# Slot attention in a decoder megakernel: the within-pair copies reordered, work moved between GpSimd and VectorE, and the lists of four engines rewritten

## The chip, the cores and the metric

The program runs on one core of one Trainium2 chip. The metric is the device time of one execution in microseconds, the median of three executions, and lower is better. A core has a matrix engine (TensorE, PE in the profile, with its weight loads as PEld), a vector engine (VectorE, DVE), an activation engine (ScalarE, ACT), a general engine (GpSimd, POOL), and SyncE (SP), whose queue issues the transfers from memory. Every engine has its own list of instructions, runs it in order, and waits for the others through semaphores. PSUM is the memory into which TensorE writes, here eight banks of 512 columns.

## What is computed

The program is two decoder layers; the change touches only the slot attention of the first. Cut to what matters:

```python
def step(carry, xs):                      # gsa2_scan, over t
    Sk, Sv = carry
    q_t, k_t, v_t, w_t, g_t, b_t = xs
    gt = jnp.exp(g_t)
    bw = b_t[:, :, None] * w_t
    Sk = Sk * gt[:, :, None, :] + k_t[..., :, None] * bw[:, :, None, :]
    Sv = Sv * gt[..., None] + bw[..., None] * v_t[:, :, None, :]
    s = jnp.einsum('bhd,bhdm->bhm', q_t, Sk) * SCALE
    a = jax.nn.softmax(s, axis=-1)
    o_t = jnp.einsum('bhm,bhmd->bhd', a, Sv)
...
q = short_conv(h @ Wq, cq)                # likewise k, v, w: 4 taps over t, then SiLU
g = jax.nn.log_sigmoid(h @ Wf1 @ Wf2)
w = l2norm(rs(w, M))
o = gsa2_scan(q, k, v, w, g, beta)
o = o * norm_w * jax.nn.sigmoid(gate)     # after a root-mean-square norm; then @ Wo
...
x = x + _L0_attn_ref(_layernorm(x, axis=-1), ...)
```

There are 64 sequences of 64 steps, 16 heads, and 128 channels and 128 slots per head.

## The kernel before, in words

The function `gsa` (from L754) holds the slot attention and takes the first 3600 us or so of the span. It goes through 16 heads with four **pairs** of token groups each, so 64 pairs. A pair has two halves, a and b, of 512 columns (eight sequences). The scan over 64 steps isn't run step by step. It is split by levels b = 1, 2, 4, 8, 16, 32: at level b the second run of b steps in each block of 2b is coupled to the first, so every level has its packed operands (P from the slot weights, G from the gates' decays), a product and a matmul. This happens twice in each half:

- **scores** (slots before the softmax): TensorE multiplies LT with AM at a level, VectorE multiplies the result in PSUM with G into TMP ("level product"), and a sum adds TMP to QK[0:512]. At levels 1, 2, 4 and 8 GpSimd does the sum (L1836, L1840, L1846, L1855 for b), at 16 and 32 VectorE (L1443, L1448). Then come transpose, maximum (L1457), its negative (nmx, L1459), Exp on ScalarE (L1715), and a custom instruction on VectorE (L1471).
- **kept attention** (after the softmax): a product AA times G gives AM at each level (VectorE L1479 to L1482 and L1487 for levels 1, 2, 8, 4, 16; GpSimd L1868 for level 32), TensorE multiplies it, and a predicated copy (L1486 to L1512 for b, L1353 to L1377 for a) puts the second runs of the result from PSUM under a mask into QK[512:1024]. Then TensorE reads the values (L1045 for a), ScalarE squares them, VectorE applies the gate (L1396), and the head's output is added to X (L1427, four instructions).

`packs`, `lefts` and `rights` are the access patterns of a level: 256 elements in the order (block, half, run of b). `rights` on QK or AA goes b elements in one region of 256, jumps to the other region, and so on; at b = 1 it jumps at every element. Besides, VectorE does the short convolutions (three instructions of 1008, 992 and 976 elements into CWV, L1399, L1405, L1415, and for CQK of 504, 496 and 488), and in-place products on GWV that prolong decays (`late`, `early`, for instance L1451 at level 2, L1433 at level 1). ScalarE starts each convolution from PSUM (L1661 for CWV), applies SiLU (L1653, L1654 into GWVa, that read CWV), packs P and G, and applies sigmoids, for which it changes its table of functions six times a pair.

The order is written out by hand. Every engine has a function `pair(h, gp, ...)` in which the statements of three pairs are interleaved: `within` (pair n, new projections), `before` (pair n-1: convolutions, gates) and `earlier` (pair n-2: scores and kept attention). The half's stages follow each other in a ring, half a pair apart. The first head and the last two pairs are unrolled; heads 1 to 15 are a loop `Fori`. SyncE loads a head's weights when the last reader of the old ones is through: WA (the four projections, 512 KB) after the last projection, WCV (taps), WFG (gates) and WO (output), each into its only buffer. The last reader of the old WA on TensorE is L1132, the first of the new one L1150. PSUM banks 0 to 3 serve half a, 4 to 7 half b.

## Time and profile before

| | |
|---|---|
| median of 3 executions | 5720.01 us (5716.29 to 5721.54) |
| the profiled execution | 5672.51 us, its span 5670.7 us |
| busy in the span: PE, DVE, ACT, POOL | 5100.0, 4610.0, 3778.8, 2229.3 us |
| granted TensorE clock | 0.97 of 2.4 GHz over the span, 0.99 from 300 to 3300 us |
| slot attention | about 80 to 3640 us of the span |

The page puts busy time beside the span for each engine; an instruction is named by its line, engine and operation, and by the tiles that it writes and reads. The profiled execution is 0.8% under the median; durations of single instructions come from it.

### The profile page before, as it was taken

The page shows a single profiled execution, that of the slowest core. Times are in us where ns is not written, and L with a number is a line of the kernel's source. Part 1 is how long each engine was busy: PE and PEld are TensorE (multiplying, and loading weights), DVE is VectorE, ACT ScalarE, POOL GpSimd, SP SyncE. Part 2 cuts the span into 40 slices and gives each one's busy share as a digit, 9 for nine tenths or more (in the row PEclk, how much of TensorE's full clock was granted, in tenths as well). Part 3 has the DMA queues.
Part 4 walks back from the last instruction along what each step waited for, and adds up shares of the span by engine and source line. Part 5 has one row for each costly group of instructions (what it writes and reads, how often), then busy time and mean ns, then how long its engine had stood idle before and what let it go on. Part 6 is the DMA issues. An engine that isn't in the chain of part 4 may idle for free. (4 is left out here: it accounts for less than half of the span.)

```text
span 5670.7 us, 113906 instructions
## 1 busy us (share of the span) xinstructions
PE 5100.0 (90%) x38178; PEld 3710.4 (65%) x38178; DVE 4610.0 (81%) x10272; ACT 3778.8 (67%) x9646; POOL 2229.3 (39%) x2774
## 2 busy tenths in 40 slices
PE   7898888988888988988988988787999999989999
PEld 4666666666666666666666666686865667768766
DVE  4999999999999999999999999687972238878623
ACT  4887787877887887877877878464861434446423
POOL 1454444554444544444544545243113320001252
PEclk9999999999999999999999999898999999999999
DMA  6300000000000000000000000001001238001134
GB/s 188 121 3 7 5 3 6 2 7 6 2 7 6 2 7 6 2 7 6 2 7 5 3 7 1 30 18 32 2 39 52 91 118 269 2 23 28 61 104 159
DMA packets 164355, 205.29 MB, mean 36 GB/s; under 512 B 22907, under 2 KB 149756, under 8 KB 163072
## 3 DMA queue, kind: packets, MB, share of 16 engines
q1 hardware_dynamic: 148016, 159.46, 9.1%
q0 software_dynamic: 12960, 34.63, 1.7%
q8 instruction: 347, 5.69, 0.4%
q10 hardware_dynamic: 2736, 3.09, 0.2%
q14 instruction: 296, 2.42, 0.1%
HBM read 158.33 MB, written 114.16 MB: 48 GB/s over the span
## 5 line engine op out<-in xcount | busy, mean ns | idle before, releaser
L1871 POOL TENSOR_TENSOR gsa_qka<-gsa_qka,gsa_tmpa 128x256 f32<-128x256 f32 x64 | 47.5, 742 | 444.5 <-DVE gsa_tmpa L1518 444.5
L1836 POOL TENSOR_TENSOR gsa_qkb<-gsa_qkb,gsa_tmpb 128x256 f32<-128x256 f32 x64 | 47.6, 744 | 443.2 <-DVE gsa_tmpb L1384 443.2
L1150 PE MATMUL PSA<-XT,gsa_wa 128*128 128x512 f32 x256 | 145.9, 700 | 51.6 <-DMA gsa_wa<-in_w_heads 51.6
L455 ACT ACTIVATE ffn0b_sl<-PSA 128x512 f32<-128x512 f32 x48 | 28.7, 597 | 207.0 <-PE PSA L162 207.0
L263 DVE TENSOR_TENSOR ffn0b_hidden<-ffn0b_sl,PSA 128x512 f32<-128x512 f32 x48 | 32.9, 686 | 163.6 <-ACT ffn0b_sl L455 163.6
L2337 POOL TENSOR_TENSOR mlstm_rs<-mlstm_wide,mlstm_neghalf 128x16 f32<-128x16 f32 x32 | 93.3, 2915 | 129.4 <-DVE mlstm_wide L2205 129.4
L1646 ACT ACTIVATE gsa_qkb<-PSA 128x512 f32<-128x512 f32 x64 | 38.2, 597 | 155.7 <-PE PSA L1032 155.7
L1621 ACT ACTIVATE gsa_caa<-PSA,gsa_nmxa 128x128 f32<-128x128 f32 x256 | 90.5, 366 | 75.2 <-DVE gsa_nmxa L1326 75.2
L1737 ACT ACTIVATE gsa_qka<-PSA 128x512 f32<-128x512 f32 x64 | 38.2, 597 | 146.7 <-PE PSA L1186 146.7
L1715 ACT ACTIVATE gsa_cab<-PSA,gsa_nmxb 128x128 f32<-128x128 f32 x256 | 90.5, 365 | 65.9 <-DVE gsa_nmxb L1459 65.9
L403 DVE COPY ffn0b_hT<-PSA 128x256 f32<-128x256 f32 x71 | 30.1, 424 | 122.2 <-PE PSA L202 122.2
L403 DVE COPY ffn1b_hT<-PSA 128x256 f32<-128x256 f32 x71 | 30.1, 424 | 121.8 <-PE PSA L202 121.8
L1008 PE MATMUL PSA<-XT,gsa_wa 128*128 128x512 f32 x256 | 125.3, 613 | 0.0
L1281 PE MATMUL PSA<-XT,gsa_wa 128*128 128x512 f32 x256 | 121.4, 597 | 3.5 <-DVE gsa_cwv L1551 3.5
L1231 PE MATMUL PSA<-gsa_wo,gsa_sgb 128*128 128x256 f32 x512 | 124.3, 387 | 0.0
L1200 PE MATMUL PSA<-gsa_qkb,gsa_gwvb 128*128 128x128 f32 x512 | 74.1, 288 | 55.0 <-DVE gsa_qkb L1512 55.0
L1161 PE MATMUL PSA<-XT,gsa_wa 128*128 128x512 f32 x256 | 121.8, 599 | 0.0
L1296 PE MATMUL PSA<-XT,gsa_wa 128*128 128x512 f32 x256 | 121.4, 597 | 0.0
L1132 PE MATMUL PSA<-XT,gsa_wa 128*128 128x512 f32 x256 | 121.3, 596 | 0.0
L1077 PE MATMUL PSA<-gsa_wo,gsa_sga 128*128 128x256 f32 x512 | 121.1, 379 | 0.0
L1054 PE MATMUL PSA<-XT,gsa_wa 128*128 128x512 f32 x256 | 120.5, 593 | 0.0
L1210 PE MATMUL PSA<-XT,gsa_wa 128*128 128x512 f32 x256 | 120.5, 593 | 0.0
(801 smaller groups left out, 19739.0 us busy)
## 6 DMA issues: line engine op xcount, KB each, us to landing
pairs<-in_blank SPq DMA_DIRECT2D x2, 35904.0 KB, 128.7
ffn0b_XS<-pairs SPq DMA_DIRECT2D x71, 132.0 KB, 2.1
ffn1b_XS<-pairs SPq DMA_DIRECT2D x71, 132.0 KB, 2.1
gsa_wa<-in_w_heads SPq DMA_DIRECT2D x16, 512.0 KB, 3.5
X<-in_x SPq DMA_DIRECT2D x8, 512.0 KB, 8.1
mlstm_CX<-in_ctx SPq DMA_DIRECT2D x32, 128.0 KB, 2.0
ffn0b_WGU<-results SPq DMA_DIRECT2D x8, 512.0 KB, 5.3
ffn0b_WD<-results SPq DMA_DIRECT2D x8, 512.0 KB, 6.6
```

The source lines that it names most:

```text
L1008: last = nc.tensor.matmul(PS[5][:, :], WA[:, c, 2 * 128:3 * 128], XT[:, c, gq * 1024 + 512:gq * 1024 + 512 + 512], start=(c == 0), stop=(c ...
L1054: last = nc.tensor.matmul(PS[6][:, :], WA[:, c, 0 * 128:1 * 128], XT[:, c, gq * 1024 + 512:gq * 1024 + 512 + 512], start=(c == 0), stop=(c ...
L1077: last = nc.tensor.matmul(PS[0 + j // 2][:, (j % 2) * 256:(j % 2) * 256 + 256], tile(SGa[:, :], j), WO[:, :], start=True, stop=True)
L1132: last = nc.tensor.matmul(PS[5][:, :], WA[:, c, 1 * 128:2 * 128], XT[:, c, gq * 1024 + 512:gq * 1024 + 512 + 512], start=(c == 0), stop=(c ...
L1150: last = nc.tensor.matmul(PS[0][:, :], WA[:, c, 3 * 128:4 * 128], XT[:, c, gp * 1024 + 0:gp * 1024 + 0 + 512], start=(c == 0), stop=(c == 1))
L1161: last = nc.tensor.matmul(PS[1][:, :], WA[:, c, 2 * 128:3 * 128], XT[:, c, gp * 1024 + 0:gp * 1024 + 0 + 512], start=(c == 0), stop=(c == 1))
L1210: last = nc.tensor.matmul(PS[2][:, :], WA[:, c, 0 * 128:1 * 128], XT[:, c, gp * 1024 + 0:gp * 1024 + 0 + 512], start=(c == 0), stop=(c == 1))
L1231: last = nc.tensor.matmul(PS[4 + j // 2][:, (j % 2) * 256:(j % 2) * 256 + 256], tile(SGb[:, :], j), WO[:, :], start=True, stop=True)
L1281: last = nc.tensor.matmul(PS[1][:, :], WA[:, c, 1 * 128:2 * 128], XT[:, c, gp * 1024 + 0:gp * 1024 + 0 + 512], start=(c == 0), stop=(c == 1))
L1296: last = nc.tensor.matmul(PS[4][:, :], WA[:, c, 3 * 128:4 * 128], XT[:, c, gp * 1024 + 512:gp * 1024 + 512 + 512], start=(c == 0), stop=(c ...
L1621: last = nc.scalar.activation(tile(CAa[:, :], j), tile(PS[3], j), ACT.Exp, bias=nmxa[:, j:j + 1], scale=SCALE, accum_out=dena[:, j:j + 1])
L2337: nc.gpsimd.tensor_tensor(rs[b][:, :], wide[b][:, :], NEGHALF[:, :], ALU.pow).then_inc(rs_by_pool, 1)
```

## The change

All of it lies in `gsa`, and what is computed stays the same.

1. **Copies in another order.** New patterns `packs_by_step`, `lefts_by_step`, `rights_by_step` name the same 256 elements, but go through one region with a step of 2b before they turn to the next: 128 elements in a run at b = 1, 64 at b = 2, 32 at b = 4. VectorE's predicated copies of levels 1, 2 and 4 use them for destination, mask and source, and so do ScalarE's packing copies of levels 1 and 2.
2. **Work between GpSimd and VectorE.** The product of kept attention of level 1 (AM[:, 0]) goes from VectorE to GpSimd, that of level 32 (AM[:, 5]) the other way. The sums of levels 4 and 8 go from GpSimd to VectorE. GpSimd keeps the sums of levels 1 and 2. A pair has 97 statements on VectorE instead of 93, 32 on GpSimd instead of 36, and 63 and 69 on TensorE and ScalarE as before.
3. **Lists and banks.** The four lists are rewritten and the PSUM banks given out anew. Half a's gate matmul and half b's value projection (columns 2*128 of WA) move from `before` to `within`; half a's softmax and its first kept products now stand at the end of a pair rather than at the start of the next one; counts of semaphores follow. `load()` on SyncE is unchanged.

The core of the diff: the new patterns, half a's copies on VectorE with the head of what follows, a moved sum, a copy at level 1, and GpSimd's list around half b's kept attention.

```diff
+            return bass.AP(t.tensor, t.offset, [t.ap[0], [b, 2], [1, b], [2 * b, 128 // b]])
+
+        def lefts_by_step(t, b):
+
+            return bass.AP(t.tensor, t.offset, [t.ap[0], [256 + b, 2], [1, b], [2 * b, 128 // b]])
+
+        def rights_by_step(t, b):
+
+            return bass.AP(t.tensor, t.offset + 256, [t.ap[0], [b - 256, 2], [1, b], [2 * b, 128 // b]])
 
         def rights1(t):
...
                         dve.sem_inc(passed_by_dve, 1)
-                        nc.vector.copy_predicated(rights(QKa[:, 512:1024], 4), packs(MASKS[:, 2, :].bitcast(I32), 4), packs(PS[0][:, 0:256], 4)).then_inc(weights_a_by_dve, 1)
+                        nc.vector.copy_predicated(rights_by_step(QKa[:, 512:1024], 4), packs_by_step(MASKS[:, 2, :].bitcast(I32), 4), packs_by_step(PS[3][:, 0:256], 4)).then_inc(weights_a_by_dve, 1)
+                        nc.vector.tensor_tensor(packs(AMa[:, 5, :], 32), rights(flat(AAa)[:, 0:512], 32), packs(Ga[:, 5, :], 32), ALU.mult).then_inc(reach_a_by_dve, 1)
                         dve.wait_ge(weights_a_by_pe, l * 6 + 4)
                         dve.wait_ge(weights_a_by_dve, l * 6 + 3)
                         dve.sem_inc(passed_by_dve, 1)
-                        nc.vector.copy_predicated(rights(QKa[:, 512:1024], 8), packs(MASKS[:, 3, :].bitcast(I32), 8), packs(PS[3][:, 0:256], 8)).then_inc(weights_a_by_dve, 1)
-                        dve.wait_ge(packed_b_by_act, l * 12 + 6)
-                        nc.vector.tensor_tensor(late(GWVb[:, 0:1024], 4), late(GWVb[:, 0:1024], 4), late_ends(GWVb[:, 0:1024], 4), ALU.mult).then_inc(decay_b_by_dve, 1)
-                        nc.vector.tensor_tensor(early(GWVb[:, 0:1024], 4), early(GWVb[:, 0:1024], 4), early_ends(GWVb[:, 0:1024], 4), ALU.mult).then_inc(decay_b_by_dve, 1)
+                        nc.vector.copy_predicated(rights(QKa[:, 512:1024], 8), packs(MASKS[:, 3, :].bitcast(I32), 8), packs(PS[0][:, 0:256], 8)).then_inc(weights_a_by_dve, 1)
                         dve.wait_ge(weights_a_by_pe, l * 6 + 5)
                         dve.wait_ge(weights_a_by_dve, l * 6 + 4)
                         dve.sem_inc(passed_by_dve, 1)
@@ -1374,134 +1346,127 @@
                         dve.wait_ge(weights_a_by_pe, l * 6 + 6)
                         dve.wait_ge(weights_a_by_dve, l * 6 + 5)
                         dve.sem_inc(passed_by_dve, 1)
-                        nc.vector.copy_predicated(rights(QKa[:, 512:1024], 32), packs(MASKS[:, 5, :].bitcast(I32), 32), packs(PS[0][:, 0:256], 32)).then_inc(weights_a_by_dve, 1)
-                    if before:
-                        dve.wait_ge(conv_a_by_dve, m * 9 + 7)
-                        nc.vector.scalar_tensor_tensor(seqs(CQK[:, 512:1024])[:, :, 2:64], seqs(PS[1][:, :])[:, :, 0:62], WCV[:, 5:6],
-                                                       seqs(CQK[:, 512:1024])[:, :, 2:64], ALU.mult, ALU.add).then_inc(conv_a_by_dve, 1)
-                    if earlier:
-                        dve.wait_ge(slots_b_by_act, l * 1 + 1)
+                        nc.vector.copy_predicated(rights(QKa[:, 512:1024], 32), packs(MASKS[:, 5, :].bitcast(I32), 32), packs(PS[1][:, 0:256], 32)).then_inc(weights_a_by_dve, 1)
+                        dve.wait_ge(packed_b_by_act, l * 12 + 4)
+                        nc.vector.tensor_tensor(late(GWVb[:, 0:1024], 2), late(GWVb[:, 0:1024], 2), late_ends(GWVb[:, 0:1024], 2), ALU.mult).then_inc(decay_b_by_dve, 1)
...
+                        nc.vector.tensor_tensor(early(GWVb[:, 0:1024], 2), early(GWVb[:, 0:1024], 2), early_ends(GWVb[:, 0:1024], 2), ALU.mult).then_inc(decay_b_by_dve, 1)
+                        nc.vector.tensor_scalar(den2a[:, :], den2a[:, :], 1e-5, None, ALU.mult).then_inc(onorm_a_by_dve, 1)
                         dve.wait_ge(onorm_a_by_act, l * 1 + 1)
-                        nc.vector.scalar_tensor_tensor(SGa[:, :], SGa[:, :], NW[:, 0:1], PS[3][:, :], ALU.mult, ALU.mult).then_inc(onorm_a_by_dve, 1)
+                        nc.vector.scalar_tensor_tensor(SGa[:, :], SGa[:, :], NW[:, 0:1], PS[1][:, :], ALU.mult, ALU.mult).then_inc(onorm_a_by_dve, 1)
...
+                        dve.wait_ge(level_b_by_dve, l * 6 + 3)
+                        dve.wait_ge(sum_b_by_pool, l * 2 + 2)
+                        nc.vector.tensor_tensor(rights(QKb[:, 0:512], 4), rights(QKb[:, 0:512], 4), packs(TMPb[:, 0, :], 4), ALU.add).then_inc(sum_b_by_dve, 1)
...
                         dve.wait_ge(weights_b_by_pe, l * 6 + 1)
-                        dve.wait_ge(diagonal_b_by_pool, l * 1 + 1)
                         dve.sem_inc(passed_by_dve, 1)
-                        nc.vector.copy_predicated(rights(QKb[:, 512:1024], 1), packs(MASKS[:, 0, :].bitcast(I32), 1), packs(PS[7][:, 0:256], 1)).then_inc(weights_b_by_dve, 1)
-                        nc.vector.tensor_tensor(packs(AMb[:, 4, :], 16), rights(flat(AAb)[:, 0:512], 16), packs(Gb[:, 4, :], 16), ALU.mult).then_inc(reach_b_by_dve, 1)
+                        nc.vector.copy_predicated(rights_by_step(QKb[:, 512:1024], 1), packs_by_step(MASKS[:, 0, :].bitcast(I32), 1), packs_by_step(PS[5][:, 0:256], 1)).then_inc(weights_b_by_dve, 1)
...
                         nc.gpsimd.tensor_tensor(tiles(QKb[:, 512:1024]), eyes4(IDENT[:, :]), columns(dcolb[:, :]), ALU.mult).then_inc(diagonal_b_by_pool, 1)
                         pool.wait_ge(softmax_b_by_act, l * 2 + 2)
-                        nc.gpsimd.tensor_tensor(packs(AMb[:, 5, :], 32), rights(flat(AAb)[:, 0:512], 32), packs(Gb[:, 5, :], 32), ALU.mult).then_inc(reach_b_by_pool, 1)
-                    if before:
+                        nc.gpsimd.tensor_tensor(packs(AMb[:, 0, :], 1), rights(flat(AAb)[:, 0:512], 1), packs(Gb[:, 0, :], 1), ALU.mult).then_inc(reach_b_by_pool, 1)
+                    if before:
+                        nc.gpsimd.tensor_tensor(packs(AMa[:, 3, :], 8), rights(CAa[:, :], 8), packs(MASKS[:, 3, :], 8), ALU.mult).then_inc(masked_a_by_pool, 1)
```

How this stands in the engines' lists is shown at three places (rows as in the program's instruction streams, from the loop over heads; REGISTER_ALU and ISA rows are bookkeeping of semaphores and pointers).

VectorE, half a, from the last predicated copies of kept attention (gsa_qka from gsa_masks and PSUM) to the first long convolution of half b (gsa_cwv). Before:

```order
L1373 COPY_PREDICATED gsa_qka<-gsa_masks,PSA 128x8x2x16
L1377 COPY_PREDICATED gsa_qka<-gsa_masks,PSA 128x4x2x32
L1379 REGISTER_ALU
L1380 SCALAR_TENSOR_TENSOR gsa_cqk<-PSA,gsa_wcv,gsa_cqk 128x8x62
L1384 TENSOR_TENSOR gsa_tmpb<-PSA,gsa_gb 128x256
L1386 REGISTER_ALU
L1387 SCALAR_TENSOR_TENSOR gsa_cqk<-PSA,gsa_wcv,gsa_cqk 128x8x61
L1391 TENSOR_TENSOR gsa_gwvb<-gsa_gwvb 128x2x16x8
L1392 TENSOR_TENSOR gsa_gwvb<-gsa_gwvb 128x2x16x8
L1394 TENSOR_TENSOR gsa_tmpb<-PSA,gsa_gb 128x256
L1396 SCALAR_TENSOR_TENSOR gsa_sga<-gsa_sga,gsa_nw,PSA 128x512
L1399 SCALAR_TENSOR_TENSOR gsa_cwv<-PSA,gsa_wcv,gsa_cwv 128x16x63
```

After:

```order
L1345 COPY_PREDICATED gsa_qka<-gsa_masks,PSA 128x8x2x16
L1349 COPY_PREDICATED gsa_qka<-gsa_masks,PSA 128x4x2x32
L1351 TENSOR_TENSOR gsa_gwvb<-gsa_gwvb 128x2x64x2
L1352 TENSOR_TENSOR gsa_tmpb<-PSA,gsa_gb 128x256
L1353 TENSOR_TENSOR gsa_gwvb<-gsa_gwvb 128x2x64x2
L1354 TENSOR_SCALAR gsa_den2a<-gsa_den2a 128x4
L1356 SCALAR_TENSOR_TENSOR gsa_sga<-gsa_sga,gsa_nw,PSA 128x512
L1359 SCALAR_TENSOR_TENSOR gsa_cwv<-PSA,gsa_wcv,gsa_cwv 128x16x63
```

Between the last copy and the convolution stood six instructions besides the gate's (gsa_sga): two short convolutions, two level products and two decay products. Now there are four besides it, all short.

ScalarE, half b's Exp (L1715 before, L1696 after; it writes gsa_cab and reads gsa_nmxb) and what stands ahead of it. Before:

```order
L1703 ACTIVATE gsa_caa<-PSA,gsa_c4a 128x128 x4
L1705 ISA
L1706 ACTIVATE gsa_pa<-gsa_gwva 128x256
L1707 ACTIVATE gsa_ga<-gsa_gwva 128x256
L1708 REGISTER_ALU
L1710 ACTIVATE gsa_gwva<-PSA,gsa_c4a 128x128 x4
L1715 ACT_TABLE_LOAD
L1715 ACTIVATE gsa_cab,gsa_denb<-PSA,gsa_nmxb 128x128 x4
```

After:

```order
L1684 ACTIVATE gsa_gb<-gsa_gwvb 128x256
L1688 ISA
L1688 ACT_TABLE_LOAD
L1688 ACTIVATE gsa_sga<-PSA,gsa_bg 128x512
L1689 REGISTER_ALU
L1691 ISA
L1692 ACTIVATE gsa_gwvb<-PSA 128x512
L1696 ACT_TABLE_LOAD
L1696 ACTIVATE gsa_cab,gsa_denb<-PSA,gsa_nmxb 128x128 x4
```

One table load stood right ahead of the Exp, behind copies and scalings; now two table loads with the two sigmoids of the gates (gsa_sga, gsa_gwvb) between them stand there. The scaling of gsa_gwva with gsa_c4a (L1710), which stood right ahead of that table load, has moved elsewhere.

TensorE, from the last matmul with the old head's gsa_wa to the first with the new one (L1132 to L1150 before, L1079 to L1123 after). Before:

```order
L1132 MATMUL PSA<-XT,gsa_wa 128x512 x2
L1137 MATMUL PSA<-IDENT,gsa_qkb 128x128 x4
L1140 ISA
L1142 MATMUL PSA<-IDENT,gsa_pa 128x128 x2
L1146 ISA
L1150 MATMUL PSA<-XT,gsa_wa 128x512 x2
```

After, first the old weights' last use, then the new ones' first:

```order
L1079 MATMUL PSA<-XT,gsa_wa 128x512 x2
L1082 REGISTER_ALU
L1084 MATMUL PSA<-gsa_amb,gsa_ltb 128x128 x2
...
L1101 MATMUL PSA<-gsa_amb,gsa_ltb 128x128 x2
L1105 MATMUL PSA<-gsa_amb,gsa_ltb 128x128 x2
L1111 MATMUL PSA<-F1T,gsa_wfg 128x512
L1113 ISA
L1115 MATMUL PSA<-IDENT,gsa_qkb 128x128 x4
L1119 ISA
L1121 ISA
L1123 MATMUL PSA<-XT,gsa_wa 128x512 x2
```

Two groups of transposes (gsa_qkb, gsa_pa) lay between the two uses; now there are nine groups of matmuls, among them those of the level products.

## Rows read from the trace of the kernel before

**Rows 1.** Windows: stretch, its us, busy (instructions) of PE, PEld, DVE, ACT, POOL; clock, DMA.
```profile
300.00:3300.00 3000.00, 2671.06 (x14289) 1891.52 (x14290) 2858.28 (x6156) 2407.07 (x6266) 1484.85 (x1869) 0.99 0.02 5
1883.50:1936.69 53.19, 48.06 (x262) 34.12 (x260) 52.13 (x113) 43.77 (x115) 26.99 (x34) 1.00 0.00 1
...
1991.08:2048.24 57.16, 49.77 (x262) 34.98 (x260) 51.62 (x113) 43.97 (x116) 27.08 (x34) 0.97 0.04 13
```

**Rows 2.** Timeline, DVE: start, duration, instruction: half a's predicated copies.
```profile
2048.24 1.26 DVE L1353 COPY_PREDICATED gsa_qka<-gsa_masks,PSA 128x256 f32<-128x256 int32 x1
...
2052.20 0.44 DVE L1373 COPY_PREDICATED gsa_qka<-gsa_masks,PSA 128x256 f32<-128x256 int32 x1
2052.77 0.44 DVE L1377 COPY_PREDICATED gsa_qka<-gsa_masks,PSA 128x256 f32<-128x256 int32 x1
2053.11 0.73 DVE L1380 SCALAR_TENSOR_TENSOR gsa_cqk<-PSA,gsa_wcv,gsa_cqk 128x496 f32<-128x496 f32 x1
```

**Rows 3.** Timeline, ACT and DVE: from those copies to the long convolution.
```profile
2055.99 1.11 ACT L1661 ACTIVATE gsa_cwv<-PSA,gsa_wcv 128x1024 f32<-128x1024 f32 x1
...
2057.13 1.27 DVE L1399 SCALAR_TENSOR_TENSOR gsa_cwv<-PSA,gsa_wcv,gsa_cwv 128x1008 f32<-128x1008 f32 x1
```

**Rows 4.** Groups by line, DVE, 300 to 3300 us: busy us, mean ns, idle before.
```profile
L1486 DVE COPY_PREDICATED gsa_qkb<-gsa_masks,PSA 128x256 f32<-128x256 int32 x55 | 69.9, 1271 | 0.0
...
L1358 DVE COPY_PREDICATED gsa_qka<-gsa_masks,PSA 128x256 f32<-128x256 int32 x55 | 38.7, 704 | 0.0
...
L1362 DVE COPY_PREDICATED gsa_qka<-gsa_masks,PSA 128x256 f32<-128x256 int32 x55 | 24.4, 444 | 7.7
...
L1443 DVE TENSOR_TENSOR gsa_qkb<-gsa_qkb,gsa_tmpb 128x256 f32<-128x256 f32 x55 | 22.6, 411 | 0.0
...
L1433 DVE TENSOR_TENSOR gsa_gwva<-gsa_gwva 128x256 f32<-128x256 f32 x55 | 22.4, 408 | 0.0
```

**Rows 5.** The same view: VectorE products that run long.
```profile
L1451 DVE TENSOR_TENSOR gsa_gwva<-gsa_gwva 128x256 f32<-128x256 f32 x55 | 82.1, 1492 | 0.0
...
L1392 DVE TENSOR_TENSOR gsa_gwvb<-gsa_gwvb 128x256 f32<-128x256 f32 x55 | 52.0, 946 | 0.0
...
L1347 DVE TENSOR_TENSOR gsa_ama<-gsa_aaa,gsa_ga 128x256 f32<-128x256 f32 x54 | 49.9, 925 | 0.0
L1346 DVE TENSOR_TENSOR gsa_ama<-gsa_aaa,gsa_ga 128x256 f32<-128x256 f32 x54 | 43.5, 806 | 2.6 <-ACT gsa_aaa L1630 2.4
...
L1439 DVE TENSOR_TENSOR gsa_gwva<-gsa_gwva 128x256 f32<-128x256 f32 x55 | 42.2, 767 | 0.0
```

**Rows 6.** Timeline, DVE and POOL: one of these products beside GpSimd.
```profile
2066.35 1.49 DVE L1451 TENSOR_TENSOR gsa_gwva<-gsa_gwva 128x256 f32<-128x256 f32 x1
...
2066.10 1.46 POOL L1859 TENSOR_TENSOR gsa_aaa<-gsa_caa,IDENT 128x512 f32<-128x512 f32 x1
```

**Rows 7.** Timeline and groups by line: the way from maximum to Exp.
```profile
2069.13 0.17 DVE L1459 TENSOR_SCALAR gsa_nmxb<-gsa_mxb 128x4 f32<-128x4 f32 x1
...
2069.33 0.37 ACT L1715 ACTIVATE gsa_cab<-PSA,gsa_nmxb 128x128 f32<-128x128 f32 x1 [1.00 <-DVE gsa_nmxb L1459]
...
L1715 ACT ACT_TABLE_LOAD x55 | 70.6, 1283 | 1.0
...
L1849 POOL TENSOR_TENSOR gsa_ssa<-gsa_ssa,gsa_neghalf 128x4 f32<-128x4 f32 x55 | 55.6, 1011 | 0.0
```

**Rows 8.** Groups by line, DVE: idle time at heads' ends; timeline, PE, weights' wait.
```profile
L1534 DVE SCALAR_TENSOR_TENSOR gsa_cwv<-PSA,gsa_wcv,gsa_cwv 128x1008 f32<-128x1008 f32 x55 | 69.7, 1267 | 11.4 <-ACT gsa_cwv L1754 11.1
...
L1479 DVE TENSOR_TENSOR gsa_amb<-gsa_aab,gsa_gb 128x256 f32<-128x256 f32 x55 | 41.6, 757 | 42.2 <-ACT gsa_aab L1724 42.2
...
L1326 DVE TENSOR_SCALAR gsa_nmxa<-gsa_mxa 128x4 f32<-128x4 f32 x55 | 9.3, 169 | 23.0 <-issue 21.6
...
2007.48 1.88 PE L1132 MATMUL PSA<-XT,gsa_wa 128*128 128x512 f32 x4
...
2013.16 3.61 PE L1150 MATMUL PSA<-XT,gsa_wa 128*128 128x512 f32 x4 [2.86 <-DMA gsa_wa<-in_w_heads]
```

926 lines of the change are left out of this document (459 added, 467 removed).

## The prediction, made before the changed kernel was run

> **What bounds the kernel now.** I read the windows first. Between 300 and 3300 us, inside slot attention, VectorE is busy 2858 of 3000 us, TensorE 2671 and GpSimd 1485, at a clock of 0.99; an undisturbed pair takes 53.19 us, 52.13 of them with VectorE busy, and the pair at a head's end 57.16 [rows 1]. So VectorE sets the pace and a microsecond off its list is a microsecond off the half, unless a wait replaces it. A half is 53.19/2 = 26.6 us, and there are 128. The timeline then shows what VectorE's time consists of, the groups by line give means, and the idle column tells where it waits today: hardly anywhere but at heads' ends. I make the sum in steps of one half, then of one head.
>
> **Copies.** Half a's copies run from 2048.24 to 2053.11, 4.87 us for six copies, one product and two decay products [rows 2]. The mean is 1271 ns at level 1, 704 at level 2, 444 at level 4, and the last of these is what 256 elements cost without trouble [rows 4]. The level 1 pattern jumps regions at each element, level 2 at each pair. The new order doesn't jump but steps by 2b. The trace has one row of a stepped operation, L1433: every operand with step 2, two of them on each element's way, and 408 ns, no more than the unstepped sum L1443 with 411 [rows 4]. So level 1 comes down to about 0.44. Levels 2 and 4 now step by 4 and 8 words, for which no row exists. Their bounds: 0.44 each (as L1362) and 1.27 each (as L1486, if a lone word is what costs). I take 0.44, since step 2 is the nearest row to a step without a jump and shows no surcharge at all. A copy directly behind another starts 0.57 after it (2052.20 to 2052.77), and other work of this size follows at 0.34 (2052.77 to 2053.11) [rows 2]. The new list has eight operations in this stretch, two of them products, and three places where copy follows copy: 3 x 0.57 + 5 x 0.34 = 3.4 us. The old one without its two decay products (moved, 0.68) and with the added product (0.34) is 4.5. That is **-1.1 per half**. ScalarE's copies in the new order hide in its own slack (44 of 53 us busy).
>
> L1358, which reads and writes adjacent pairs, already takes 704 ns, while L1433, with single words at step 2, takes 408 [rows 4]: here the jump costs, not the lone word. The Trainium skill ("Vector Engine (DVE) Microarchitecture Reference", section 5.2) speaks against this change: it has a port stream at full rate only if consecutive elements come in runs of at least two adjacent words, and gives about 2.5 ns a column where a side steps farther each time. By that an estimate is 256 x 2.5 + 75 = 0.72 us for each of the three copies, and the sum below would be some 0.84 us a half, or 107 us, higher. At step 2 the trace disagrees with it; at 4 and 8 nothing here tells.
>
> **Moved sums.** Two sums of 411 ns [rows 4] at a pace of 0.33 start to start: **+0.66 per half**. The exchange of products (level 1 for level 32) leaves the count alike.
>
> **GpSimd in VectorE's way.** Five products that should take 0.41 have means of 1492, 946, 925, 806 and 767 ns [rows 5]: 2.9 us of excess per half. The timeline shows what it is: L1451 starts at 2066.35 and runs until 2067.84, 0.28 us after the end of GpSimd's L1859 (2066.10, 1.46 long) [rows 6], so it did its work in those 0.28 us and stood before. A VectorE product with both sources in SBUF stands still while GpSimd works; those that read PSUM don't. The new list puts most decay products between convolutions and the copies, where GpSimd is idle or I find only short overlaps: the sum of level 8 beside GpSimd's multiplication with c4a, 0.25, and the kept products beside the diagonal, 0.4 or so. With 0.7 kept, **-2.2 per half**. Bounds: all 2.9 gone, or 1.5 kept.
>
> **First new wait: the long convolution.** From the last copy (2052.77, [rows 2]) TensorE reads the values, ScalarE applies SiLU, squares, then starts the convolution from PSUM into the tile that SiLU just read (2055.99, 1.11 long), and VectorE's follows at 2057.13 [rows 3]. That is 4.36 us, which VectorE fills today without a gap. In the new list this stretch holds the copy and three products (4 x 0.34), a four-column operation (0.3) and the gate's 512 columns (half of L1399's 1.27 [rows 3], 0.7) = 2.4: **+2.0 per half** idle. What is queued behind is all of VectorE's list. If ScalarE gets there sooner the wait is 1.3, if the square or the matmuls are later it is 2.8.
>
> **Second new wait: Exp.** Today the negative maximum is out at 2069.13 and Exp starts at 2069.33, after ScalarE idled 1.00 [rows 7]. Now, ahead of Exp, there stand two table loads of 1.28 [rows 7] and two sigmoids, and ahead of these a scaling that waits for GpSimd's c4a: two powers of 1.01 (the row of L1849 [rows 7]), a mask product and the scaling itself. Counting from the first copy in the new list, I get Exp at 19.4 and the negative maximum at 18.9: **+0.5 per half**. This is the least certain term: 0 to 1.3.
>
> The half: 26.6 - 1.1 + 0.66 - 2.2 + 2.0 + 0.5 = **26.5 us**, 0.1 less; times 128, **-13 us**. TensorE (48.06 a pair [rows 1]) would not bind before 24.0.
>
> **Heads' ends.** In 13 heads VectorE waited 42.2 us at L1479 and 11.1 at L1534, 4.1 us a head [rows 8]. The first goes back to WA: TensorE ends its last matmul with the old ones (L1132) at 2009.36, and starts the first with the new ones (L1150) at 2013.16, after idling 2.86 [rows 8]; the load took at most 3.8. In the new list the old weights' last use and the new ones' first use are nine groups of matmuls apart, nine groups of 0.5 to 1 us, an estimate of 5.2 us from TensorE's mean load in a half, and so more than the load needs. WCV too is asked for some 6 us before ScalarE needs it. The gates' weights get a tight place at L1259 but at most 0.5 us, under which TensorE has slack. The loop's own 21.6 us (L1326, issue) stay. So 4.1 x 15 = **-61 us**. If the load is late by a microsecond still, -46.
>
> Together -74 on the profiled execution's 5672.5; I carry the difference over to the median of 5720, which lies 0.8% above it: **5646 us**.
>
> **Rivals.**
> A, the forecast, 5646: as above.
> B, steps of 4 and 8 cost what jumping in pairs costs, 0.70. Level 2 gains nothing and level 4 loses 0.26: +0.52 x 128 = +67, 5713. For it speaks that no row excludes it.
> C, fewer waits: ScalarE comes to the convolution 0.5 earlier, as no decay packs lie ahead of it, and Exp does not wait; half 25.9, so -90 - 61, 5569. For it: ScalarE and TensorE have 9 and 5 us of slack a pair.
> D, the other side: the Exp on ScalarE. If the scaling with c4a, which sits behind two powers and a mask product on GpSimd, lets the two table loads start 0.8 later than I count, VectorE idles that much more in each half: 27.3, +90 - 61, 5749. It decides from +0.58 a half (74/128) on. For it: 6.7 us of ScalarE and GpSimd work in a chain where today there are 3; against it: VectorE has two short convolutions as filler between the maximum and the custom instruction.
> E, lone words cost what they do at level 1 today, 1.27 at levels 2 and 4: +1.66 x 128 = +212, 5858. Break-even at 0.58 a half for both copies together, so 0.73 us each. L1433 speaks against it.
> The skill's 0.72 for all three copies lands between B and D, at 5753; in the chances it is part of D's end.
>
> **Numbers.** A 0.44, B 0.13, C 0.15, D 0.16, E 0.12. A measurement of this kernel can tell about 0.2% (11 us) from no change. Faster by more than that: nearly all of A (0.41), C, and parts of B and D (0.07) = 0.63. Slower: E, most of D and a bit of B = 0.27. Within 0.2%: 0.10. The range leaves out E and C's far end: 5560 to 5775.
>
> **What would show it.** In the changed kernel's groups by line the predicated copies of levels 1, 2 and 4 (L1455, L1459, L1464) should each be at 440 ns; 700 means B, 1270 means E. The long convolution (L1359) should have idle time of some 2 us each, released by ScalarE. The custom instruction after Exp should have 0.5. No product of VectorE should be over 0.8 us on average. TensorE should show no wait for gsa_wa. An undisturbed pair should take 53.0 us and a head 4 x 53.0 + 1.7. If the copies are as forecast and the pair is still above 53.8, one of the two new waits was sized wrongly; if the pair is under 52.2, both were oversized or the GpSimd excess was larger than its five rows.

## The result and the profile after

The changed kernel takes **6166.51 us** (median of four, 6164.44 to 6174.32) against 5718.69 us before: a ratio of **1.0785** (95% interval 1.0767 to 1.0804), so it is 448 us slower. The prediction was 5646 us with a range of 5560 to 5775: wrong in sign and outside the range. The profiled execution took 6166.15 us, so times of the profile can be used as they are.

The first row below is the stretch from 300 to 3300 us, which answers to [rows 1]; the others are half b's copies (1952.00) and then half a's (1920.00 and 1923.10), with what follows them to the long convolution and behind it (windows of the changed kernel: stretch, its us, busy us and count of PE, PEld, DVE, ACT, POOL, then the granted clock as a share of 2.4 GHz, the DMA share and GB/s).

```profile
300.00:3300.00 3000.00, 2594.37 (x12639) 1800.02 (x12638) 2507.50 (x5643) 2168.01 (x5544) 1176.59 (x1458) 0.92 0.02 4
1952.00:1956.45 4.45, 2.00 (x14) 1.42 (x12) 4.06 (x7) 1.50 (x2) 0.00 (x0) 1.00 0.00 0
1920.00:1923.10 3.10, 1.67 (x13) 1.28 (x11) 2.97 (x6) 2.66 (x5) 0.25 (x1) 1.00 0.00 0
1923.10:1926.00 2.90, 2.30 (x8) 1.71 (x8) 2.27 (x5) 0.00 (x0) 0.00 (x0) 0.56 0.00 0
1926.00:1931.30 5.30, 4.77 (x15) 3.21 (x16) 2.79 (x6) 2.66 (x5) 2.92 (x4) 0.60 0.00 0
1931.30:1936.00 4.70, 4.23 (x30) 3.73 (x28) 4.38 (x7) 3.68 (x16) 1.24 (x2) 1.00 0.00 0
```

VectorE, which had 2858 of these 3000 us busy, has 2507 now: it no longer sets the pace alone. TensorE's clock is 0.92 instead of 0.99, and it isn't evenly lower: in 1923.10 to 1931.30, the end of half a's copies and what follows them, it is 0.56 to 0.60 (mean of stretches at 1.2 and at 2.4 GHz), and 1.00 in the rows at 1952.00 and 1931.30. TensorE was busy for 1.67 of the 3.10 us ahead of the fall (row at 1920.00) and for 2.00 of 4.45 in half b's copies, behind which the clock stayed. Half b of this pair is the exception: single instructions of the window show TensorE's read of the values (L1019, L1171) slowed in 81 of 97 halves. 3000 us hold 49 pairs instead of 55.

VectorE's groups by line (busy us, mean ns, idle before and its releaser), which answer to [rows 4] and [rows 5]:

```profile
L1592 DVE COPY_PREDICATED gsa_qka<-gsa_masks,PSA 128x256 f32<-128x256 int32 x49 | 63.1, 1288 | 6.5
...
L1336 DVE COPY_PREDICATED gsa_qka<-gsa_masks,PSA 128x256 f32<-128x256 int32 x49 | 60.0, 1224 | 26.7 <-issue 17.2 <-PE PSA L1011 9.5
...
L1451 DVE TENSOR_TENSOR gsa_amb<-gsa_aab,gsa_gb 128x256 f32<-128x256 f32 x48 | 45.8, 954 | 0.0
...
L1455 DVE COPY_PREDICATED gsa_qkb<-gsa_masks,PSA 128x256 f32<-128x256 int32 x48 | 34.8, 724 | 0.0
```

The stepped copies cost 724 ns at level 1 (L1455), 1288 at level 2 (L1592) and 1224 at level 4 (L1336), where I had put 440 for each.

TensorE's row of work between the copies and behind them (timeline, PE: start, duration, instruction, idle time before), and its groups by line:

```profile
1923.23 1.07 PE L1011 MATMUL PSA<-gsa_ama,gsa_pa 128*128 128x128 f32 x4 [1.49 <-DVE gsa_ama L1593]
...
1926.53 2.07 PE L1019 MATMUL PSA<-gsa_qka,gsa_gwva 128*128 128x128 f32 x8 [0.67 <-DVE gsa_qka L1349]
...
1954.07 0.71 PE L1163 MATMUL PSA<-gsa_amb,gsa_pb 128*128 128x128 f32 x4 [1.49 <-DVE gsa_amb L1460]
```
```profile
L1025 PE MATMUL PSA<-XT,gsa_wa 128*128 128x512 f32 x196 | 144.9, 884 | 0.0
...
L1019 PE MATMUL PSA<-gsa_qka,gsa_gwva 128*128 128x128 f32 x392 | 94.1, 416 | 37.3 <-DVE gsa_qka L1349 37.3
L1079 PE MATMUL PSA<-XT,gsa_wa 128*128 128x512 f32 x196 | 93.2, 598 | 0.1
```

TensorE waits 1.49 us for VectorE's product (L1593) that is queued behind a dear copy, and in half a then works at the low clock: L1019, the read of the values, has a mean of 416 ns where the same read took 288 before, and L1025 884 where the same shape at full clock (L1079) takes 598. Half b waited the same 1.49 us (L1460) and kept its clock, so the length of this one wait doesn't decide it, and what does isn't shown. But the two halves, side by side with the same lists and the same copies, show what the low clock costs VectorE at the gate (timeline, DVE, half a at the low clock, half b at the full one):

```profile
1930.31 0.75 DVE L1356 SCALAR_TENSOR_TENSOR gsa_sga<-gsa_sga,gsa_nw,PSA 128x512 f32<-128x512 f32 x1 [2.23 <-ACT gsa_qka L1626]
...
1959.81 0.75 DVE L1486 SCALAR_TENSOR_TENSOR gsa_sgb<-gsa_sgb,gsa_nw,PSA 128x512 f32<-128x512 f32 x1 [1.31 <-ACT gsa_qkb L1724]
```

That is 0.92 us more in the half with the low clock. What the engines wait for (engine, line, waited for: us in total, times, longest):

```profile
DVE gsa_sga L1356 <- ACT gsa_qka L1626: 101.8, 49, 2.2
...
DVE gsa_wta L1569 <- ACT gsa_caa L1792: 44.1, 49, 0.9
...
DVE gsa_cwv L1359 <- ACT gsa_cwv L1630: 12.7, 49, 0.3
```

Both new waits of the prediction are here, the first mostly one step ahead of where I had put it: 101.8/49 = 2.08 us at the gate (L1356) and only 0.26 at the long convolution (L1359) directly behind it, and 0.90 at the custom instruction after Exp (L1569).

### The profile page after: what moved, and what is told of

Its sections match the earlier page's. It is cut to its first block and busy times, and to the rows that moved or that the text cites. A ratio compares the mean times of both kernels' runs of the same rounds, so it can differ in the third digit from the quotient of the medians.

```text
span 6164.4 us, 113783 instructions
## 1 busy us (share of the span) xinstructions
PE 5409.5 (88%) x38178; PEld 3879.6 (63%) x38178; DVE 4584.6 (74%) x10528; ACT 3825.4 (62%) x9645; POOL 2049.8 (33%) x2518
## 5 line engine op out<-in xcount | busy, mean ns | idle before, releaser
L1025 PE MATMUL PSA<-XT,gsa_wa 128*128 128x512 f32 x256 | 187.4, 876 | 0.0
L1177 PE MATMUL PSA<-XT,gsa_wa 128*128 128x512 f32 x256 | 174.6, 822 | 0.9 <-DVE gsa_tmpa L1481 0.9
L1019 PE MATMUL PSA<-gsa_qka,gsa_gwva 128*128 128x128 f32 x512 | 124.7, 420 | 48.4 <-DVE gsa_qka L1349 48.4
L1845 POOL TENSOR_TENSOR gsa_r4a<-gsa_r0a,gsa_neghalf 128x4 f32<-128x4 f32 x64 | 64.9, 1015 | 272.4 <-DVE gsa_r0a L1372 272.4
L1171 PE MATMUL PSA<-gsa_qkb,gsa_gwvb 128*128 128x128 f32 x512 | 113.8, 392 | 46.7 <-DVE gsa_qkb L1477 46.7
L1877 POOL TENSOR_TENSOR gsa_r4b<-gsa_r0b,gsa_neghalf 128x4 f32<-128x4 f32 x64 | 64.9, 1015 | 270.0 <-DVE gsa_r0b L1505 270.0
L1011 PE MATMUL PSA<-gsa_ama,gsa_pa 128*128 128x128 f32 x256 | 51.0, 328 | 115.9 <-DVE gsa_ama L1593 73.6
L1356 DVE SCALAR_TENSOR_TENSOR gsa_sga<-gsa_sga,gsa_nw,PSA 128x512 f32<-128x512 f32 x64 | 47.8, 747 | 133.6 <-ACT gsa_qka L1626 133.6
L1019 PEld LDWEIGHTS PSA<-gsa_qka,gsa_gwva 128*128 128x128 f32 x512 | 106.3, 308 | 64.2 <-DVE gsa_qka L1349 64.2
L1486 DVE SCALAR_TENSOR_TENSOR gsa_sgb<-gsa_sgb,gsa_nw,PSA 128x512 f32<-128x512 f32 x64 | 47.8, 748 | 124.2 <-ACT gsa_qkb L1724 124.2
L1171 PEld LDWEIGHTS PSA<-gsa_qkb,gsa_gwvb 128*128 128x128 f32 x512 | 96.4, 281 | 62.1 <-DVE gsa_qkb L1477 62.1
L1163 PE MATMUL PSA<-gsa_amb,gsa_pb 128*128 128x128 f32 x256 | 49.8, 321 | 94.4 <-DVE gsa_amb L1460 94.3
L1123 PE MATMUL PSA<-XT,gsa_wa 128*128 128x512 f32 x256 | 122.3, 601 | 8.9 <-DMA gsa_wa<-in_w_heads 8.9
```

The source lines that it names most:

```text
L1019: last = nc.tensor.matmul(tile(PS[1], j), tile(GWVa[:, 1024:1536], j), tile(QKa[:, 512:1024], j), start=True, stop=True)
L1025: last = nc.tensor.matmul(PS[7][:, :], WA[:, c, 0 * 128:1 * 128], XT[:, c, gq * 1024 + 512:gq * 1024 + 512 + 512], start=(c == 0), stop=(c ...
L1123: last = nc.tensor.matmul(PS[1][:, :], WA[:, c, 2 * 128:3 * 128], XT[:, c, gp * 1024 + 0:gp * 1024 + 0 + 512], start=(c == 0), stop=(c == 1))
L1171: last = nc.tensor.matmul(tile(PS[5], j), tile(GWVb[:, 1024:1536], j), tile(QKb[:, 512:1024], j), start=True, stop=True)
L1177: last = nc.tensor.matmul(PS[3][:, :], WA[:, c, 0 * 128:1 * 128], XT[:, c, gp * 1024 + 0:gp * 1024 + 0 + 512], start=(c == 0), stop=(c == 1))
L1845: nc.gpsimd.tensor_tensor(r4a[:, :], r0a[:, :], NEGHALF[:, :], ALU.pow).then_inc(onorm_a_by_pool, 1)
```

## The experiments

All ratios are to the kernel before, measured beside each run on the same chip (medians of 5668.5 to 5671.2 us), with their 95% interval; differences in us are worked out from the ratios. In what follows a kernel "of before" or "of after" is that kernel with the edit shown.

### Which copies in which order

The first run keeps the stepped order at level 1 alone in the changed kernel (half b's copies; half a's likewise):

```diff
-nc.vector.copy_predicated(rights_by_step(QKb[:, 512:1024], 2), packs_by_step(MASKS[:, 1, :].bitcast(I32), 2), packs_by_step(PS[6][:, 0:256], 2))
+nc.vector.copy_predicated(rights(QKb[:, 512:1024], 2), packs(MASKS[:, 1, :].bitcast(I32), 2), packs(PS[6][:, 0:256], 2))
...
-nc.vector.copy_predicated(rights_by_step(QKb[:, 512:1024], 4), packs_by_step(MASKS[:, 2, :].bitcast(I32), 4), packs_by_step(PS[7][:, 0:256], 4))
+nc.vector.copy_predicated(rights(QKb[:, 512:1024], 4), packs(MASKS[:, 2, :].bitcast(I32), 4), packs(PS[7][:, 0:256], 4))
```

> The changed kernel, with VectorE's predicated copies of levels 2 and 4 put back into the old order; level 1 keeps the stepped one. In the profile of the changed kernel the stepped copies took 1289 and 1224 ns (levels 2 and 4), the old ones 704 and 444. Theory 1 (price of the stepped copies alone): 1.36 us less in each of 128 halves, 6166 - 174 = 5992. Theory 2 (the dear copies also let TensorE idle and so cost clock, which dropped to 0.6 behind them and made the read of the values 416 instead of 288 ns and the next projection 884 instead of 593): the clock comes back too, another 0.13 x 8 + 0.29 x 4 = 2.2 us of TensorE per half, of which about half is in the chain to the long convolution, so 5830 to 5880. Theory 3 (the new lists themselves cost most): the waits at the gate (2.0 us a half) and at Exp (0.9) stay, and the time stays above 5950.

Measured: 5765.43 us, ratio 1.0169 (1.0153 to 1.0186). Four instructions a pair put back give 6.2% (1.0785 to 1.0169), 352 us, or 2.75 us a half. That is twice their own surcharge of 1.36 us, so theory 1 alone is out and theory 2 holds, somewhat more strongly than I had put it: the window's clock is back at 0.98, and the gate waits 1.31 us in an undisturbed pair. Theory 3 is out as a main cause; of its waits the one after Exp stays at 0.9, and 1.7% above before remain with the new lists.

The other two put the stepped order into the kernel before, at level 1 alone and at levels 1, 2 and 4 (shown for half a's level 1, the others likewise):

```diff
-nc.vector.copy_predicated(rights(QKa[:, 512:1024], 1), packs(MASKS[:, 0, :].bitcast(I32), 1), packs(PS[3][:, 0:256], 1))
+nc.vector.copy_predicated(rights_by_step(QKa[:, 512:1024], 1), packs_by_step(MASKS[:, 0, :].bitcast(I32), 1), packs_by_step(PS[3][:, 0:256], 1))
```

> The kernel before, with only VectorE's predicated copies of level 1 in the stepped order (724 ns in the changed kernel's profile against 1271). Theory: VectorE sets the pace there, so 0.55 x 128 = 70 us less, 5650. Rival: what follows the copy waits for TensorE's next product anyway, and the time stays within 0.2% of 5719.

> The kernel before, with VectorE's predicated copies of levels 1, 2 and 4 in the stepped order, as the changed kernel has them; lists and everything else as before. If the copies' own price is all they do: -0.55 + 0.58 + 0.78 = +0.81 us a half, 5719 + 104 = 5823. If the copies also cost TensorE its clock in the stage after them, as in the changed kernel: above 5900.

Measured: level 1 alone 5610.44 us, ratio **0.9892** (0.9875 to 0.9909); all three 5778.51 us, ratio 1.0190 (1.0173 to 1.0207). In the old lists the copies do about what their price says: -61 us where 70 were expected, +108 where 104 were. The difference between the two kernels, 0.0298 x 5670 = 169 us, is 1.3 us a half for the copies of levels 2 and 4. The window of 300 to 3300 us of the second shows that TensorE nearly keeps its clock there, at 0.98:

```profile
300.00:3300.00 3000.00, 2624.69 (x13856) 1863.73 (x13855) 2858.56 (x5971) 2337.61 (x6073) 1433.91 (x1810) 0.98 0.02 5
```

So the same two copies cost 1.3 us a half in the old lists and 2.75 in the new ones. The reads of the values take 288 and 325 ns there (L1057, L1212), against 416 and 399 in the changed kernel. In the old lists TensorE's products stand further ahead of VectorE's copies: in half b it waits 0.38 us before the last of them (L1208) and 1.44 before the read, where it waits 1.49, 0.68 and 0.68 in the new ones (medians of the window). That this is why the clock holds wasn't tested by itself.

### What a copy costs

A list of single operations, three times each with nothing beside them, put ahead of the kernel before (RS and PT are the stepped patterns, FL a contiguous one):

```diff
...
+for _ in range(3): go(nc.vector.copy_predicated(RS(D[:, 512:1024], 4), FL(M[:, 0:256].bitcast(I32), 4), FL(PSA[:, 0, 0:256], 4)))
...
+for _ in range(3): go(nc.vector.copy_predicated(FL(D[:, 0:256], 4), PT(M[:, 0:256].bitcast(I32), 4), FL(PSA[:, 0, 0:256], 4)))
...
+for _ in range(3): go(nc.vector.copy_predicated(FL(D[:, 0:256], 4), FL(M[:, 0:256].bitcast(I32), 4), PT(PSA[:, 0, 0:256], 4)))
...
```

> The kernel before with a list of single copies and products ahead of it, each three times with nothing beside it, on tiles of its own: the predicated copy of 128x256 contiguous, jumping (old order) at levels 1, 2, 4, 8, stepped (new order) at levels 1 to 16, and with only destination, only mask or only the PSUM source stepped; products of 128x256 with one source, the destination or all stepped; ScalarE's copies in both orders. Theory 1: a step beyond 2 words is dear on whichever SBUF side it lies (one side about 0.72 us, several sides 1.2). Theory 2: only the predicated copy's destination, which must be read and written, is dear, and products stay near 0.41 at steps of 4 and 8.

The lines, by their numbers: 3872 all contiguous; 3873 to 3875 the old order at levels 1, 2, 4; 3877 to 3880 the stepped order at levels 1, 2, 4, 8; 3882 to 3884 only the destination stepped (steps of 2, 4, 8 words); 3887 only the mask (8); 3890 only the PSUM source (8). Groups by line, DVE:

```profile
L3878 DVE COPY_PREDICATED bench_d<-bench_m,PSA 128x256 f32<-128x256 int32 x3 | 3.9, 1290 | 0.1
L3883 DVE COPY_PREDICATED bench_d<-bench_m,PSA 128x256 f32<-128x256 int32 x3 | 3.9, 1285 | 0.1
...
L3880 DVE COPY_PREDICATED bench_d<-bench_m,PSA 128x256 f32<-128x256 int32 x3 | 3.8, 1264 | 0.1
L3873 DVE COPY_PREDICATED bench_d<-bench_m,PSA 128x256 f32<-128x256 int32 x3 | 3.8, 1251 | 0.1
...
L3879 DVE COPY_PREDICATED bench_d<-bench_m,PSA 128x256 f32<-128x256 int32 x3 | 3.7, 1225 | 0.1
L3884 DVE COPY_PREDICATED bench_d<-bench_m,PSA 128x256 f32<-128x256 int32 x3 | 3.7, 1222 | 0.1
...
L3877 DVE COPY_PREDICATED bench_d<-bench_m,PSA 128x256 f32<-128x256 int32 x3 | 2.2, 722 | 0.1
L3882 DVE COPY_PREDICATED bench_d<-bench_m,PSA 128x256 f32<-128x256 int32 x3 | 2.2, 721 | 0.1
L3874 DVE COPY_PREDICATED bench_d<-bench_m,PSA 128x256 f32<-128x256 int32 x3 | 2.1, 716 | 0.1
...
L3887 DVE COPY_PREDICATED bench_d<-bench_m,PSA 128x256 f32<-128x256 int32 x3 | 1.8, 615 | 0.1
...
L3875 DVE COPY_PREDICATED bench_d<-bench_m,PSA 128x256 f32<-128x256 int32 x3 | 1.3, 441 | 0.1
...
L3890 DVE COPY_PREDICATED bench_d<-bench_m,PSA 128x256 f32<-128x256 int32 x3 | 1.3, 441 | 0.1
L3872 DVE COPY_PREDICATED bench_d<-bench_m,PSA 128x256 f32<-128x256 int32 x3 | 1.3, 441 | 0.1
```

Among the three operands the destination makes the price: with only it stepped the copy costs what it costs with all three (721, 1285, 1222 ns). A mask stepped by itself adds 0.17 us (615 ns, L3887) and nothing on top of a stepped destination, the PSUM source nothing. Both orders follow one count, that of **words per 16 bytes of destination**, which means how many consecutive elements fall into the same 16 bytes: four in a row (contiguous, old order at level 4) 441 ns; two (old order at level 2, stepped at level 1) 716 and 722; one (old order at level 1, stepped from level 2 on) 1251, 1290, 1225, 1264. From 441 to 716 to 1251 it is, as an estimate, about 4.2 ns for each of 64, 128, 256 visits to a place of 16 bytes, over some 0.17 us. Why it is 16 bytes isn't shown by this, only that this count orders all of the rows. Theory 2 holds for the predicated copy, but for the 0.17 of the mask.

Products are another matter (line 3894 contiguous, 3896 and 3897 one source at steps 4 and 8, 3899 the destination at 4, 3902 all three at 4), and so are ScalarE's copies (3916 old order at level 2, 3917 to 3919 stepped at levels 1, 2, 4):

```profile
L3918 ACT ACTIVATE bench_d<-bench_e 128x256 f32<-128x256 f32 x3 | 2.0, 651 | 0.1
...
L3899 DVE TENSOR_TENSOR bench_d<-bench_e 128x256 f32<-128x256 f32 x3 | 1.8, 612 | 0.1
L3902 DVE TENSOR_TENSOR bench_d<-bench_e 128x256 f32<-128x256 f32 x3 | 1.8, 612 | 0.1
...
L3896 DVE TENSOR_TENSOR bench_d<-bench_e 128x256 f32<-128x256 f32 x3 | 1.8, 608 | 0.1
...
L3916 ACT ACTIVATE bench_d<-bench_e 128x256 f32<-128x256 f32 x3 | 1.3, 442 | 0.1
...
L3894 DVE TENSOR_TENSOR bench_d<-bench_e 128x256 f32<-128x256 f32 x3 | 1.3, 425 | 0.1
```

0.61 us instead of 0.42 at steps of 4 and 8 words, whatever is stepped: the second part of theory 2, that products stay at 0.41, is wrong. My row for the prediction, L1433 at step 2, was an in-place product [rows 4]: it stood for neither the operation nor the step. The Trainium skill ("Vector Engine (DVE) Microarchitecture Reference", section 5.2) has hops between regions at every element at 1.71 to 1.98 ns a column, and 2.50 for steps of 24 words, the row that the prediction carried over to steps of 2, 4 and 8. With the section's slope of 1.04 ns a column, steps of 4 and 8 words in a product come to an estimate of (608 - 425) / 256 + 1.04 = 1.75 here, near the former. The predicated copy's destination comes to (1285 - 441) / 256 + 1.04 = 4.3 ns, far above either, and the hop between runs of two adjacent words, which the section has as free, is not free for it (716 against 441).

### What made the dear copies twice as dear

TensorE does two of the kept attention's groups more than once, the same product into the same bank, where it idles between the copies:

```diff
-                        for e in range(2):
+                        for e in (0, 1) * 3:
                             last = nc.tensor.matmul(tile(PS[4][:, 0:256], e), tile(Pb[:, 3, :], e), tile(AMb[:, 3, :], e), start=True, stop=True)
...
-                        for e in range(2):
+                        for e in (0, 1) * 2:
                             last = nc.tensor.matmul(tile(PS[6][:, 0:256], e), tile(Pb[:, 4, :], e), tile(AMb[:, 4, :], e), start=True, stop=True)
```

> The changed kernel, in which TensorE does the kept attention's matmuls of level 8 three times instead of once and those of level 16 twice, for both halves, always the same product into the same bank, just where it idles between VectorE's dear copies (1.49 and 0.68 us in the profile of the changed kernel). The output is the same; TensorE has 1.8 us more work a half. Theory 1 (the idling itself costs, since TensorE's clock falls to 0.6 behind it, and with it the read of the values and the projection in the chain to the gate): the clock stays at 1.0, the read comes from 416 back to 288 ns, and the program gets faster although it does more, by 1 us or so a half: about 0.98 of the changed kernel, ratio to before 1.05 to 1.06. Theory 2 (idle and clock are a mere sign of VectorE's delays): the same as the changed kernel or slower, ratio 1.079 to 1.10.

Measured: 5906.15 us, ratio **1.0409** (1.0392 to 1.0426), where the changed kernel has 1.0785. With more work the kernel is 3.5% faster (1.0409 / 1.0785), 1.7 us a half; theory 1, and more than the 1 us that I had expected. Windows and TensorE's groups of this kernel:

```profile
300.00:3300.00 3000.00, 2690.87 (x14524) 1922.05 (x14522) 2607.71 (x5929) 2270.19 (x5823) 1220.10 (x1533) 0.98 0.02 4
1900.00:1957.00 57.00, 51.13 (x277) 36.27 (x278) 49.38 (x115) 42.66 (x110) 23.33 (x29) 1.00 0.04 13
```
```profile
L1177 PE MATMUL PSA<-XT,gsa_wa 128*128 128x512 f32 x204 | 96.0, 593 | 0.0
...
L1163 PE MATMUL PSA<-gsa_amb,gsa_pb 128*128 128x128 f32 x408 | 59.1, 288 | 31.2 <-DVE gsa_amb L1460 31.2
L1171 PE MATMUL PSA<-gsa_qkb,gsa_gwvb 128*128 128x128 f32 x408 | 59.1, 288 | 39.8 <-DVE gsa_qkb L1477 39.8
```

The clock is back at 0.98 (1.00 in an undisturbed pair), half b's read (L1171) at 288 ns and the projection (L1177) at 593. An undisturbed pair takes 56.97 us, 28.5 a half, where no pair of the changed kernel's loop takes less than 58.43 (means with the heads' ends: 58.7 here, 61.6 there). What is left above the first experiment's 27.2 is 1.3 a half, as much as the copies' own price in the old lists. The Trainium skill ("Advanced Engine Details and Errata", section Clock Domains) says that the array's clock is gated to 1.2 GHz when idle. These rows agree that idling costs the clock, and add that here a row of short waits could be enough, with TensorE still busy for 1.67 of the 3.10 us ahead of the fall.

### The division between GpSimd and VectorE

The kernel before with stepped copies at level 1, and the sums of levels 4 and 8 on VectorE:

```diff
+dve.wait_ge(level_b_by_dve, l * 6 + 3)
+dve.wait_ge(sum_b_by_pool, l * 2 + 2)
+nc.vector.tensor_tensor(rights(QKb[:, 0:512], 4), rights(QKb[:, 0:512], 4), packs(TMPb[:, 0, :], 4), ALU.add).then_inc(sum_b_by_dve, 1)
...
-pool.wait_ge(level_b_by_dve, l * 6 + 3)
-nc.gpsimd.tensor_tensor(rights(QKb[:, 0:512], 4), rights(QKb[:, 0:512], 4), packs(TMPb[:, 0, :], 4), ALU.add).then_inc(sum_b_by_pool, 1)
...
```

> The kernel before with stepped copies at level 1 (ratio 0.989 before) and the sums of levels 4 and 8 moved from GpSimd to VectorE as in the change; GpSimd keeps those of levels 1 and 2. Theory 1, as in the prediction's sum: two sums at 0.33 a half, +0.66, less what GpSimd's two sums took from VectorE through the port, so between +0.3 and +0.66 a half, +38 to +85 us, ratio 0.996 to 1.004. Rival: GpSimd's sums held up VectorE's in-place products (L1451, L1439, L1392) for more than that, since GpSimd then does its long product earlier: no change or faster than 0.989.

Measured: 5619.24 us, ratio 0.9908 (0.9891 to 0.9924); without the moved sums it was 0.9892. The difference is 9 us, and the two intervals overlap (their far ends are 28 us apart), where the sum of the prediction has 0.66 x 128 = 84 before relief for VectorE's products. Theory 1 asked for at least 38, so the rival is nearer: GpSimd's sums had held up VectorE's products by about what they cost. The rows of VectorE's products (against [rows 5]) say where it went:

```profile
L1466 DVE TENSOR_TENSOR gsa_gwva<-gsa_gwva 128x256 f32<-128x256 f32 x56 | 83.6, 1492 | 0.0
...
L1463 DVE TENSOR_TENSOR gsa_qkb<-gsa_qkb,gsa_tmpb 128x256 f32<-128x256 f32 x56 | 29.0, 519 | 1.9
...
L1366 DVE TENSOR_TENSOR gsa_ama<-gsa_aaa,gsa_ga 128x256 f32<-128x256 f32 x55 | 25.3, 460 | 0.0
...
L1455 DVE TENSOR_TENSOR gsa_gwva<-gsa_gwva 128x256 f32<-128x256 f32 x56 | 22.9, 408 | 0.0
```

L1455 is the product of level 1 that had 767 ns (L1439 before) and has 408; L1463 has 519 (L1448 before: 606) and L1366 460 (L1354 before: 626). That is 0.36 + 0.09 + 0.17 = 0.62 us a half, about the price of the two sums. L1466 keeps its 1492, against what the rival said of it: in the timeline it starts at 1818.38, and GpSimd's product with the identity (L1873) runs from 1818.14 to 1819.59. Moving an addition away from GpSimd was free here within the intervals, and no gain.

### ScalarE's stepped copies

The changed kernel with stepped copies at level 1 only, on ScalarE too (level 2 costs it 692 ns stepped, in the list above 651 against 442):

```diff
-nc.scalar.activation(packs_by_step(Pa[:, 1, :], 2), lefts_by_step(GWVa[:, 512:1024], 2), ACT.Copy)
+nc.scalar.activation(packs(Pa[:, 1, :], 2), lefts(GWVa[:, 512:1024], 2), ACT.Copy)
...
```

> The changed kernel with stepped copies at level 1 alone, on VectorE and now also on ScalarE (whose stepped copy of level 2 costs 651 ns against 442 in the price list; four of them a pair). Before, with ScalarE's level 2 still stepped, the ratio was 1.017. Theory 1 (ScalarE's list up to Exp is in the chain, 0.9 us of wait a half): 0.2 to 0.4 a half less, ratio 1.008 to 1.012. Theory 2 (ScalarE is off the path there, the wait at Exp comes from the two table loads and VectorE's own maximum): ratio stays at 1.016 to 1.018.

Measured: 5754.71 us, ratio 1.0152 (1.0133 to 1.0171), against 1.0169 (1.0153 to 1.0186). The intervals overlap; an undisturbed pair went from 54.35 to 54.31 us, and the wait at the custom instruction stayed at 0.9 us. Theory 2: ScalarE's copies are off the path, as far as these intervals tell (its range began at 1.016).

### The jump back of the loop

In the first experiment's kernel undisturbed pairs take 54.35 us, but the pair before and the one after the loop's jump 57.3 and 58 to 60. DVE and PE at the jump (timeline), and the windows behind it:

```profile
2040.22 0.44 DVE L1336 COPY_PREDICATED gsa_qka<-gsa_masks,PSA 128x256 f32<-128x256 int32 x1 [2.48 <-issue]
...
2046.80 0.75 DVE L1356 SCALAR_TENSOR_TENSOR gsa_sga<-gsa_sga,gsa_nw,PSA 128x512 f32<-128x512 f32 x1 [2.23 <-ACT gsa_qka L1626]
```
```profile
2040.27 1.22 PE L1011 MATMUL PSA<-gsa_ama,gsa_pa 128*128 128x128 f32 x4 [3.40 <-issue]
```
```profile
2028.00:2038.00 10.00, 8.59 (x44) 5.71 (x42) 8.59 (x23) 7.87 (x21) 3.06 (x4) 1.00 0.02 4
...
2041.00:2044.00 3.00, 2.33 (x11) 2.03 (x10) 2.26 (x7) 0.00 (x0) 0.31 (x1) 0.50 0.00 0
2044.00:2048.00 4.00, 4.00 (x10) 2.12 (x9) 1.52 (x3) 2.88 (x6) 2.61 (x4) 0.50 0.02 4
2048.00:2054.00 6.00, 5.45 (x35) 4.66 (x34) 4.27 (x8) 4.16 (x17) 2.75 (x4) 0.91 0.01 1
```

The new lists put the jump between two copies of half a's kept attention. TensorE idles 3.40 us, VectorE 2.48, and the clock falls from 1.00 to 0.50 until 2048: the gate (L1356) then waits 2.23 us instead of 1.31. The edit writes the loop as five passes of three heads (here VectorE's list; the others alike), for this kernel and for the fastest one (below):

```diff
-                with dve.Fori(1, 16) as h:
-                    for gp in range(4):
-                        pair(h, gp)
+                with dve.Fori(0, 5) as i:
+                    for k in range(3):
+                        for gp in range(4):
+                            pair(i * 3 + (1 + k), gp)
```

> The changed kernel with stepped copies at level 1 alone (ratio 1.017), and the loop over heads 1 to 15 written as five passes of three heads instead of fifteen of one: ten of the fifteen jumps back are gone, every engine's list is otherwise the same. In its profile the jump fell into half a's row of copies: TensorE idle 3.4 us, VectorE 2.5, and then 10 us at clock 0.5 with longer waits at the gate (2.23 for 1.31), at the packs (1.73 for 0) and at the maximum (0.80 for 0). Theory 1 (the jump and the slow clock behind it are the dear part of a head's end): the pairs at 57.3 and 58 to 60 us come down to 54.5 in ten heads, about 6 us a head, -60 us, ratio 1.006. Theory 2 (it is the load of the weights, as in the kernel before): no more than the 1.5 us of the jump itself, -15 us, ratio 1.014.

Measured: 5707.16 us, ratio 1.0068 (1.0051 to 1.0085), from 1.0169: 57 us for ten jumps, 5.7 us each; theory 1. Only every third head now has pairs of 57.3 and 58 us.

### A version that beats both

Each copy in the order that the list makes cheap, on the lists of before: level 1 stepped on both engines, level 2 in adjacent pairs, a region at a time:

```diff
+        def rights_by_half(t, b):
+            return bass.AP(t.tensor, t.offset + 256, [t.ap[0], [b - 256, 2], [2 * b, 128 // b], [1, b]])
...
-nc.vector.copy_predicated(rights(QKa[:, 512:1024], 2), packs(MASKS[:, 1, :].bitcast(I32), 2), packs(PS[2][:, 0:256], 2))
+nc.vector.copy_predicated(rights_by_half(QKa[:, 512:1024], 2), packs_by_half(MASKS[:, 1, :].bitcast(I32), 2), packs_by_half(PS[2][:, 0:256], 2))
...
-nc.scalar.activation(packs(Ga[:, 0, :], 1), rights(GWVa[:, 0:512], 1), ACT.Copy)
+nc.scalar.activation(packs_by_step(Ga[:, 0, :], 1), rights_by_step(GWVa[:, 0:512], 1), ACT.Copy)
```

> The kernel before with every copy in the order that the price list makes cheap: level 1 stepped on VectorE and on ScalarE (there 427 ns against 551 and 528 in the profile of before), and level 2 in runs of two adjacent words with a step of four words in one region, region after region, on both engines. Theory 1 (a jump between regions costs, adjacent pairs don't): the copy of level 2 falls from 704 to 441 ns, 0.26 a half, ratio 0.989 - 0.006 = 0.983. Theory 2 (what costs is the number of separate places in the destination, however near): level 2 stays at 704 or so and the ratio at 0.989.

Measured: 5601.21 us, ratio 0.9874 (0.9858 to 0.9891), against 0.9892 for level 1 on VectorE alone; the intervals overlap. Level 1 stepped (L1377) costs the 0.72 of the list, and level 2 by region (L1382) costs what it did:

```profile
L1377 DVE COPY_PREDICATED gsa_qka<-gsa_masks,PSA 128x256 f32<-128x256 int32 x56 | 40.6, 724 | 4.7 <-PE PSA L1037 4.6
...
L1382 DVE COPY_PREDICATED gsa_qka<-gsa_masks,PSA 128x256 f32<-128x256 int32 x56 | 40.1, 715 | 0.0
```

L1382, level 2 without the jump between regions at each pair but still with two words per 16 bytes, has 715 ns: it is not the jump that costs, and theory 2 holds again. The same kernel with five passes of three heads:

> The fastest kernel so far (the kernel before with each copy in its cheap order, ratio 0.987), with the same loop of five passes of three heads. There VectorE waited 21.4 us at the jump in 14 heads and 45.8 for the load of WA. Theory 1: 1.5 us for ten jumps, -15 us, ratio 0.985. Theory 2 (the longer body costs as much in fetching instructions as the jumps did): unchanged at 0.987.

Measured: 5585.68 us, ratio **0.9851** (0.9835 to 0.9868), 1.5% faster than the kernel before and 8.7% faster than the changed one. By the ratios the ten jumps give 13 us, by the medians 15, and the intervals of this run and the one before it overlap. The traces decide for theory 1: VectorE's idle time at the jump (groups by line, 250 to 3500 us) falls from 21.4 us (L1350) to 6.3 (L1351), 1.5 us for each of ten jumps. That is a quarter of what a jump costs in the new lists. Here it lies in front of nmx (the negative maximum), not in the row of copies.

## Why the prediction was wrong, point by point

**What bounds the kernel: right for before, and dropped too early for after.** In the kernel before, 0.55 us off VectorE's list gave 0.48 a half (61 us over 128), as [rows 1] had it. But the sum treated TensorE as covered up to 24 us a half. At full clock its busy time does fit under the half (49.1 us of 54.35 in an undisturbed pair of the first experiment's kernel), but its clock didn't stay: 0.92 in place of 0.99. This is one of the steps that failed: the sum has no term for what VectorE's copies do to TensorE's clock.

**Copies: -1.1 predicted, +0.8 measured.** The other step that failed, and the larger one, is "I take 0.44, since step 2 is the nearest row to a step without a jump": the copies of levels 1, 2 and 4 took 0.72, 1.29 and 1.22. The rival E (lone words cost 1.27 at levels 2 and 4) was right about the price and had a chance of 0.12; its time, 5858, still lacked the clock. The evidence was in [rows 4]: the copy of level 2, with adjacent pairs, took 704 ns where L1433, a product, showed no surcharge at step 2. I read this as "the jump costs, not the lone word", though the two rows differ in the operation as well. Compared with copies alone (1271, 704, 444 at one, two and four adjacent words), a dependence on adjacency explains the three rows as well as one on jumps, and it makes levels 2 and 4 dear. The Trainium skill's rule that the prediction quotes pointed the same way, though its 0.72 a copy is too low for levels 2 and 4, and the 5753 that follows from it lies above both B and D, not between them. Together with the idle and the clock the step is worth 128 x (0.8 + 1.1) = 243 us of the miss, and another 128 x (2.75 - 1.3) = 186 for what it does to TensorE.

**Moved sums +0.66 and GpSimd out of VectorE's way -2.2: the sum of them is about right.** The run with the moved sums shows that the two cost 0.07 together with their relief, within the intervals. In the changed lists VectorE's product of 1492 ns is gone, and one of 954 (L1451) stays, which my sign of no product above 0.8 us had ruled out. The terms' sum can only be had by difference: 1.1 us a half for the lists as a whole (next point) less the waits of 1.6 and 0.9 leaves -1.4, where I had -1.5.

**The two new waits: about right in size at full clock, the first mostly at the gate instead of the convolution.** In the first experiment's kernel, in an undisturbed pair, the gate waits 1.31 and the convolution 0.26, 1.6 where I had 2.0 at the convolution, and the custom instruction 0.9 where I had 0.5. The lists as a whole, once the copies are alike, cost 54.35 against 52.15 us a pair (first experiment against the kernel before with stepped level 1), so 1.1 us a half; the terms of the prediction without the copies, 0.66 - 2.2 + 2.0 + 0.5, give 0.96. That the sum agrees so closely is partly luck: the two waits were off by 0.4 each, in opposite directions. Rival D asked for 0.8 more at Exp: it was 0.4.

**Heads' ends: -4.1 us a head predicted, about +2 measured.** A head's four pairs exceed four undisturbed ones by 1.9 + 3.9 = 5.8 us in the kernel before (55.1 and 57.1 against 53.2) and by 0.35 + 2.95 + 4.5 = 7.8 in the first experiment's (54.7, 57.3 and about 58.9 against 54.35); in the changed kernel itself the clock hides where a head ends. The part on WA was right: no wait for it is left in the loop. The 4.1 were to be gained against before, and the cost rose by 2 instead. Two things were overlooked. The jump, which I let stand at 1.7 us, had moved into the row of copies, where both engines need each other; with the clock behind it, it costs 5.7 us (the run with three heads a pass). And the gates' weights, "at most 0.5 us", are waited for 0.9 to 1.0 us a head:

```profile
PE PSA L1259 <- DMA gsa_wfg<-in_w_gates: 11.9, 13, 1.0
```

**Adding up.** From the prediction of 5646: +243 (copies), +186 (their effect on TensorE), (4.1 + 2) x 15 = +92 (heads' ends) and 128 x 0.14 = +18 (lists) give 6185, against 6166 measured. The terms come from different runs and overlap a little, since the clock is low at heads' ends anyway; that they meet to 19 us is partly luck.

**By kernels.** Level 1 stepped -1.1%, the new lists and the new division +2.8% (0.9892 to 1.0169), levels 2 and 4 stepped +6.2%, about half of it their own time and half that of TensorE at its low clock.

## What to carry to other kernels

Price an access pattern by a row of the same operation. For a predicated copy, count how many consecutive words it writes into the same 16 bytes, not its jumps: the best order for one level was the worst for the next two. If the engine that sets the pace slows down in a short exchange with TensorE, ask what TensorE's clock does in the stage behind it; if busy work in the gap makes a kernel faster, the clock was part of it. When lists are rotated, look at where the loop's jump falls: between independent stages it cost 1.5 us here, inside an exchange 5.7.

## What the hardware showed that I had not expected

- A predicated copy's price goes by its destination, 441, 716 and 1251 ns for 256 elements with four, two and one word per 16 bytes; its PSUM source could be stepped at no cost (441), a mask stepped alone cost 615.
- TensorE's granted clock fell to 0.5 to 0.6 (1.2 GHz for most of the time) from 1923.10 to 1931.30, in and behind a row of copies in which TensorE waited 1.5 us and less at a time. It did so in most halves but not in all: half b at 1952 had the same wait of 1.49 us and kept 1.00. Repeating matmuls that nobody needed made the kernel 3.5% faster.
- A product of 256 elements on VectorE costs 0.61 us instead of 0.42 at steps of 4 and 8 words, whether one operand is stepped or all.
- ScalarE's copies cost 651 instead of 442 ns when stepped by 4 words, and 427 when stepped by 2.
